# A recurrence's output gate in a PSUM bank and an activation of its own, with the 1 + o operation waiting for that activation, on one core

## What is computed

```python
x = x + L0_conv(ln_c(x))     # 7x7 involution: per-position kernels from two 1x1 convolutions
t = to_tokens(x);  t = t + L0_ffn(ln_t(t))   # 16 experts (64 -> 128 -> 64), the top 2 weighted
x = from_tokens(t);  x = x + L1_conv(ln_c(x))  # 3x3 convolution composed from low-rank terms
t = to_tokens(x);  t = t + L1_ffn(ln_t(t))   # a recurrence over the 3136 tokens:

def step(carry, xs):
    h, c = carry                      # each (4, 64)
    xi_t, xf_t, xg_t, xo_t = xs       # x_t @ U + b for every gate
    i_t = sigmoid(xi_t + h @ V_i)
    g_t = tanh(xg_t + h @ V_c)
    o_t = sigmoid(xo_t + h @ V_o)
    c_new = h * c + i_t * g_t         # gate f is not used
    h_new = o_t * tanh(c_new)
    return (h_new, c_new), h_new
```

## Time and profile before

| | |
|---|---|
| time, median of three | 3995.21 us |
| the profiled execution, its time | 3996.03 us |
| its span, first to last instruction | 3994.3 us |
| PE busy | 3584.6 us (90%) |
| DVE (VectorE) busy | 3374.4 us (84%) |
| ACT (ScalarE) busy | 2527.2 us (63%) |
| POOL (GpSimd) busy | 2156.5 us (54%) |
| recurrence steps | 3136 |

### The profile page before, as it was taken

The page is one execution under the profiler, slowest core; times in us unless marked ns, Lnnn a source line. Parts: engine busy times, 40 slices in busy tenths (PEclk is TensorE's granted clock), DMA queues, the critical chain, the costliest instruction groups (busy, mean ns, idle before and its releaser), DMA issues.

```text
span 3994.3 us, 130407 instructions
## 1 busy us (share of the span) xinstructions
PE 3584.6 (90%) x35548; PEld 2659.6 (67%) x35548; DVE 3374.4 (84%) x21816; ACT 2527.2 (63%) x11668; POOL 2156.5 (54%) x3179
## 2 busy tenths in 40 slices
PE   6899999989899999999999999999989899988888
PEld 5666666666666666666666666666666666666665
DVE  6688888888888888888888888888888888888887
ACT  4366666666666666666666666666666666666565
POOL 6655565656565656555555555565655565652222
PEclk7955555555555555555555555555555555555555
DMA  5000000000000000000000000000000000000000
GB/s 74 2 1 1 1 1 1 1 1 1 1 1 1 1 1 1 1 1 1 1 1 1 1 1 1 1 1 1 1 1 1 1 1 1 1 2 1 1 1 1
DMA packets 44538, 11.06 MB, mean 3 GB/s; under 512 B 39914, under 2 KB 44011, under 8 KB 44491
## 3 DMA queue, kind: packets, MB, share of 16 engines
q1 hardware_dynamic: 42378, 10.05, 1.6%
q10 hardware_dynamic: 2112, 0.46, 0.1%
HBM read 7.29 MB, written 3.21 MB: 3 GB/s over the span
## 4 chain that ended last, share of the span: by engine, by line
PE 66%; DVE 14%; ACT 13%; issue 5%; POOL 1%; DMA 0%; DVEq 0%; ACTq 0%; POOLq 0%
PE GATES L1343 14%; PE YB L1163 10%; PE GATES L1413 9%; ACT O L747 7%; PE H1B L1157 7%; ACT G L743 6%; DVE O L998 6%; PE YB L1314 6%; PE TAPB L1150 6%; PE DB L1282 5%; DVE HR L1002 5%; PE DB L1144 3%; PE H2B L1190 1%; PE H1B L1190 1%; PE H2B L1138 1%
## 5 line engine op out<-in xcount | busy, mean ns | idle before, releaser
L743 ACT ACTIVATE G<-GATES 128x12 f32<-128x12 f32 x3136 | 571.1, 182 | 1206.8 <-PE GATES L1413 1195.2
L1413 PEld LDWEIGHTS GATES<-HR,VW 128*128 128x128 f16 x6272 | 421.4, 107 | 601.5 <-issue 556.7
L1343 PE MATMUL GATES<-HR,VW 128*128 128x4 f16 x3136 | 531.8, 170 | 306.9 <-DVE HR L1002 214.0
L989 DVE TENSOR_TENSOR_SCAN CT<-G,CT 128x12 f32<-128x12 f32 x3136 | 586.5, 187 | 247.8 <-ACT G L743 218.7
L747 ACT ACTIVATE O<-G 128x8 f32<-128x8 f32 x3136 | 663.2, 211 | 98.7 <-ACT G L743 0.2
L998 DVE RECIPROCAL O<-O 128x4 f32<-128x4 f32 x3136 | 568.3, 181 | 175.1 <-ACT O L747 0.3
L1409 PEld LDWEIGHTS <-VW 128*128 128x128 f16 x3136 | 457.3, 146 | 354.3 <-issue 317.7
L976 DVE SCALAR_TENSOR_TENSOR CT<-HIST,CT 128x4 f32<-128x4 f32 x3136 | 522.0, 166 | 126.9 <-DVE HIST L1008 13.1
L1413 PE MATMUL GATES<-H,VB 128*128 128x4 f16 x6272 | 619.3, 169 | 0.0
L1413 PE MATMUL GATES<-HR,VW 128*128 128x4 f16 x6272 | 614.5, 168 | 0.0
L1163 PE MATMUL YB<-HD,W 128*64 128x112 f32 x3840 | 596.0, 412 | 1.7 <-DVE HD L869 1.7
(11 more groups left out here) (245 smaller groups left out, 6993.2 us busy)
## 6 DMA issues: line engine op xcount, KB each, us to landing
out_dram<-OUT SPq DMA_DIRECT2D x112, 28.0 KB, 1.9
X<-in_x_dram SPq DMA_DIRECT2D x4, 672.0 KB, 10.9
STG<-in_L_ffn_w_dram SPq DMA_DIRECT2D x4, 512.0 KB, 12.7
U<-in_L_conv_U2s_dram SPq DMA_DIRECT2D x1, 972.0 KB
W<-in_L_ffn_w_dram SPq DMA_DIRECT2D x1, 512.0 KB, 12.0
X<-in_x_dram ACTq DMA_DIRECT2D x4, 112.0 KB, 3.2
S<-in_L_conv_S1s_dram SPq DMA_DIRECT2D x1, 108.0 KB
S<-in_L_conv_S2s_dram SPq DMA_DIRECT2D x1, 108.0 KB
```

The costliest lines, as they stand in the source:

```text
L743: act.activation(G6[:, :, 2:5], gates[c][:, w, :, :], ACT.Tanh, scale=1 / GSCALE).then_inc(step_in, 1)
L989: dve.tensor_tensor_scan(CELL.rearrange("z b k -> z (b k)"), G6[:, :, :].rearrange("z b k -> z (b k)")[:, 0::2], ADD3.rearrange("z b k -> ...
L1343: return pe.add_instruction(mybir.InstMatmult(name=nc.get_next_instruction_name(), engine=mybir.EngineType.PE, start_tensor_calc=False, st ...
L1413: last = pe.matmul(gates[c][:, w, :, SLOT[g]], wt[:, g].rearrange("z m c -> z (m c)"), digit, start=False, stop=True, skip_group_check=True)
```

## The change

Gate o leaves the shared bank. Its inputs and its recurrent matmuls go into GATE_O, two slices of 112 columns of bank DB, in place of the third slice of GATES[0] and [1]; the order of the matmuls for each part of h becomes g, i, o (SLOT = (1, 0)). gates_done now counts after i, gate_o_done after o. ScalarE's L743 takes g and i alone (8 elements). A new activation takes tanh(o), 4 elements, from GATE_O to OT, four columns of the same bank, after the count step_in that stood ahead of L747 and after gate_o_done; 1 + o reads OT and waits for ot_done. Gate o's inputs are filled in by three prefills at place 5 for the second half of the row and at place 54 for the next row's first half, after 1 + o of that place (o1_done); the other six stand at place 3 and at places 51 to 53. As the prefill into DB no longer clears the bank in these rows, ScalarE zeroes a slice at places 1 and 49, and the first o matmul of the next place waits for it. The experts' weights move from DB into H1B, where expert H1 then waits for their copy (dbs_done) instead of for SI, and the spread norm factors move into H2B.

```diff
--- before.py
+++ after.py
...
         GAT=0, IXF=3, DM=((4, 5), (6, 8)), DT=(8, 9), DP=10, DPLO=11, DUPX=44, X4=47, DUP=54, XS=55, OUT3=54, OUT2=53,
-        PRE0={51: (0, 1, 2), 52: (3, 4), 53: (5, 6), 54: (7, 8)}, COPY=None, RSE=None)
+        PRE0={51: (0, 1), 52: (2, 3), 53: (4, 5)}, PRE0_O={54: (6, 7, 8)}, COPY=None, RSE=None)
 def head_places():
...
         GAT=0, IXF=0, DM=((0, 0), (0, 0)), DT=(1, 1), DP=2, DPLO=3, DUPX=50, X4=51, DUP=53, XS=54, OUT3=54, OUT2=54,
-        PRE0={55: tuple(range(9))}, COPY=5, RSE=23)
+        PRE0={55: tuple(range(9))}, PRE0_O={}, COPY=5, RSE=23)
 OUT_FREE_AT = (13, 48)
-PRODUCTS = 3 + 2 * 3
-PRE1_AT = {3: (0, 1, 2, 3, 4), 6: (5, 6, 7, 8)}
-SLOT = (2, 0, 1)
+INPUTS = (("b", 0), ("b", 1), (0, 0), (0, 1), (1, 0), (1, 1), ("b", 2), (0, 2), (1, 2))
+PRODUCTS = len(INPUTS)
+FIRST_O = INPUTS.index(("b", 2))
+PRE1_AT = {3: (0, 1, 2, 3, 4, 5), 5: (6, 7, 8)}
+ZERO_AT = (1, 49)
+SLOT = (1, 0)
 MAIN, HEAD = main_places(), head_places()
...
         TC5 = CT[:, 32:52].rearrange("z (b k) -> z b k", k=5)
-        gates = [g[:, 0:HALF * B * 3].rearrange("z (k b t) -> z t b k", b=B, k=3) for g in GATES]
+        gates = [g[:, 0:HALF * B * 2].rearrange("z (k b t) -> z t b k", b=B, k=2) for g in GATES]
+        GATE_O = [DB[:, c * TOK:(c + 1) * TOK] for c in range(2)]
+        gate_o = [g.rearrange("z (b t) -> z t b", b=B) for g in GATE_O]
+        OT = DB[:, 448:448 + B]
         REDF = TAPB[64:96, TOK:2 * TOK]
...
         def spread(lstm):
-            return DB if lstm else GATES[1]
+            return H2B if lstm else GATES[1]
+        def weights_bank(lstm):
+            return H1B if lstm else DB
         def logits(lstm):
...
                 act.wait_ge(hd_done, 1 + NG * j + k)
-                act.activation(DBS[:, :], DB[:, 0:EG * 2 * TOK], ACT.Copy).then_inc(dbs_done, 1)
+                act.activation(DBS[:, :], weights_bank(lstm)[:, 0:EG * 2 * TOK], ACT.Copy).then_inc(dbs_done, 1)
         def act_registers(act, j, t, involution):
...
             n = (j - LAG) * W + t
-            act.to_reg(1 + n + 1)
             if t < W - 1:
                 act.to_reg(1 + n + 2)
+                act.to_reg(1 + 2 * n + 4)
             if t == P.SQ:
...
                     act.wait_ge(gates_done, 1 + n + 1)
-                    act.activation(G6[:, :, 2:5], gates[c][:, w, :, :], ACT.Tanh, scale=1 / GSCALE).then_inc(step_in, 1)
+                    act.activation(G6[:, :, 2:5:2], gates[c][:, w, :, :], ACT.Tanh, scale=1 / GSCALE).then_inc(step_in, 1)
+                    act.wait_ge(step_in, 1 + 2 * n + 2)
+                    act.wait_ge(gate_o_done, 1 + n + 1)
+                    act.activation(OT[:, :], gate_o[c][:, w, :], ACT.Tanh, scale=1 / GSCALE).then_inc(ot_done, 1)
                     act_registers(act, j, t, involution)
-                    act.wait_ge(step_in, 1 + 2 * n + 2)
-                    act.activation(O5[:, :, 1:5:3], G6[:, :, 3:4].broadcast_to([128, B, 2]), ACT.Copy, scale=O_MAX, bias=1.0)\
-                        .then_inc(o1_done, 1)
+                    act.wait_ge(ot_done, 1 + n + 1)
+                    act.activation(O5[:, :, 1:5:3], OT[:, :].unsqueeze(2).broadcast_to([128, B, 2]), ACT.Copy, scale=O_MAX,
+                                   bias=1.0).then_inc(o1_done, 1)
                     act.wait_ge(cell_done, 1 + n + 1)
...
                         .then_inc(t_done, 1)
+                    for k in range(2):
+                        if t == ZERO_AT[k]:
+                            act.wait_ge(o1_done, 1 + n + 1)
+                            act.activation(GATE_O[1 - k], CST[:, CZERO:CZERO + 1].broadcast_to([128, TOK]), ACT.Copy).then_inc(oz_done, 1)
                 act_fill(act, j, t, involution, lstm, experts, pre)
...
-        def prefill(pe, c, k):
-            if k < 3:
-                return pe.matmul(GATES[c][:, SLOT[k] * TOK:(SLOT[k] + 1) * TOK], BX[:, k].rearrange("z m c -> z (m c)"),
-                                 ONEH[:, :], start=(k == 0), stop=False, skip_group_check=True)
-            d, g = divmod(k - 3, 3)
+        def prefill(pe, c, k, lstm):
+            d, g = INPUTS[k]
+            bank = GATE_O[c] if g == 2 else GATES[c][:, SLOT[g] * TOK:(SLOT[g] + 1) * TOK]
+            if d == "b":
+                return pe.matmul(bank, BX[:, g].rearrange("z m c -> z (m c)"), ONEH[:, :],
+                                 start=(k == 0 or (k == FIRST_O and not lstm)), stop=False, skip_group_check=True)
             xs = X4S[:, :].rearrange("z (p q w) -> z p q w", p=2, q=Q)[:, :, :, c * HALF:(c + 1) * HALF]
-            return pe.matmul(GATES[c][:, SLOT[g] * TOK:(SLOT[g] + 1) * TOK].rearrange("z (q p t) -> z p q t", q=Q, p=2),
+            return pe.matmul(bank.rearrange("z (q p t) -> z p q t", q=Q, p=2),
                              UX[:, d, g].rearrange("z m c -> z (m c)"), xs, start=False, stop=False, skip_group_check=True)
...
                         if lstm:
-                            pe.wait_ge(dbs_done, 1 + NG * j)
+                            pe.wait_ge(ve_done, 1 + 2 * j + 2)
                     last = spread_rs(pe, spread(lstm), 2 * k, 2 * k + 2)
...
                         pe.wait_ge(step_in, 1 + 2 * (j - LAG) * W)
-                    last = prefill(pe, 1, k)
+                    if k == FIRST_O:
+                        pe.wait_ge(o1_done, 1 + (j - LAG) * W + t + 1)
+                    last = prefill(pe, 1, k, lstm)
                     if k == PRODUCTS - 1:
...
                 k = P.H1.index(t)
-                pe.wait_ge(si_done, 1 + NG * j + k)
+                if lstm:
+                    pe.wait_ge(dbs_done, 1 + NG * j + k)
+                else:
+                    pe.wait_ge(si_done, 1 + NG * j + k)
                 if k == 0 and lstm:
...
                 if k == 0 and lstm:
-                    pe.wait_ge(ve_done, 1 + 2 * j + 2)
+                    pe.wait_ge(rsc_done, 1 + j + 1)
                 pe.wait_ge(v_done, 1 + 2 * NG * j + 2 * k)
...
                 if k == 0:
-                    if lstm:
-                        pe.wait_ge(rsc_done, 1 + j + 1)
                     pe.wait_ge(dp_step, 1 + 3 * j + 3)
...
                     for p in range(2):
-                        last = pe.matmul(DB[:, (2 * m + p) * TOK:(2 * m + p + 1) * TOK], SEL[:, p, EG * k + m, :], DP[:, :],
+                        last = pe.matmul(weights_bank(lstm)[:, (2 * m + p) * TOK:(2 * m + p + 1) * TOK], SEL[:, p, EG * k + m, :], DP[:, :],
                                          start=(m == 0 and p == 0), stop=True, skip_group_check=True)
...
                         pe.wait_ge(x4_done, 1 + j + 1)
-                    last = prefill(pe, 0, k)
+                    last = prefill(pe, 0, k, lstm)
                     if k == PRODUCTS - 1:
...
             if t == P.DUP:
-                if experts:
+                if experts and lstm:
+                    pe.wait_ge(dbs_done, 1 + NG * (j + 1))
+                elif experts:
                     pe.wait_ge(si_done, 1 + NG * (j + 1))
...
                     duplicate(pe, GATES[0], XD4).then_inc(dupx_done, 1)
+                for k in P.PRE0_O.get(t, ()):
+                    if k == FIRST_O:
+                        pe.wait_ge(o1_done, 1 + (j - LAG) * W + t + 1)
+                    last = prefill(pe, 0, k, lstm)
+                    if k == PRODUCTS - 1:
+                        last.then_inc(pre0_done, 1)
         def multiply_loaded(pe, out, weights, moving):
...
                         multiply_loaded(pe, gates[c][:, w, :, SLOT[0]], first, digit)
-                        for g in range(1, 3):
-                            last = pe.matmul(gates[c][:, w, :, SLOT[g]], wt[:, g].rearrange("z m c -> z (m c)"), digit,
-                                             start=False, stop=True, skip_group_check=True)
-                    last.then_inc(gates_done, 1)
+                        last = pe.matmul(gates[c][:, w, :, SLOT[1]], wt[:, 1].rearrange("z m c -> z (m c)"), digit,
+                                         start=False, stop=True, skip_group_check=True)
+                        if wt is VB:
+                            last.then_inc(gates_done, 1)
+                        if wt is VW and t - 1 in ZERO_AT:
+                            pe.wait_ge(oz_done, 1 + 2 * (j - LAG) + ZERO_AT.index(t - 1) + 1)
+                        last = pe.matmul(gate_o[c][:, w, :], wt[:, 2].rearrange("z m c -> z (m c)"), digit,
+                                         start=False, stop=True, skip_group_check=True)
+                    last.then_inc(gate_o_done, 1)
                 pe_fill(pe, j, t, involution, lstm, experts, pre)
...
```

More of the change, by code:

```diff
@@ L50 @@
 Places = namedtuple("Places", """MEAN MEAN_ORDER XC SQ VAR VE RSB RSC CONV1 RELU RED H1 SI H2 DB VV DBS HD W3 TAPA PA TAPD PROD CONV
-LOGIT LG MAX IDX NM TANH PW GAT IXF DM DT DP DPLO DUPX X4 DUP XS OUT3 OUT2 PRE0 COPY RSE""")
+LOGIT LG MAX IDX NM TANH PW GAT IXF DM DT DP DPLO DUPX X4 DUP XS OUT3 OUT2 PRE0 PRE0_O COPY RSE""")
 def main_places():
@@ L278, in build_program @@
```

(12 more changed lines are left out.)

## The result

The changed kernel takes 4318.89 us, the median of four runs (4316.59 to 4321.93), against 3995.23 (3995.12 to 3996.76). The ratio is 1.0811, 95% interval 1.0797 to 1.0824: 324 us slower. The forecast was 4282.

A forecast was written before the change was run, and what follows sets the result against it. The bound was 3136 turns of one serial loop, gates, cell, h, gates. Later L1005 0.117 less one matmul 0.026 gave 0.091 a turn, +285 us; with + 3, + 3 and - 4, 4282 us, range 4238 to 4385.

The forecast's parts named there:

- reserve on the o path: VectorE, before the change: the reciprocal's result is in at 0.675, L1005 starts at 0.71 behind HR; 0.035 us spare.
- The new last wait: VectorE: the reciprocal instead of HR releases L1005, which moves from 0.706 to 0.823, 0.117 us later a turn.
- the 0.82 ns an element: ScalarE: slope taken from L703 and L743, shortening L743 from 182 to 178.5 ns with 8 elements instead of 12.
- the bound of 1 + o: ScalarE: 1 + o taken as 178 ns, bounds 167 and 211; at 211 it adds 33 ns a turn, 4385 us.
- Tanh(o)'s own bound of 182 ns: ScalarE: tanh(o) from PSUM to PSUM taken as 158.5 ns, bounds 155 and 182.
- the second count's 0.03: ScalarE: tanh(o)'s second wait, gate_o_done, was put at nothing, with a bound of 0.03 us.
- Banks, prefills, H1's wait: PE and the bank work: bank moves and H1's wait cost nothing, prefills at places 5 and 54 3 us.
- VectorE's RED: VectorE's filler makes the next scan 0.09 late, 0.03 more x 50 rows; with DPLO + 3 us.
- A: ScalarE: tanh(o) starts 0.07 behind L743 without waiting for its end; -0.03 a turn, 3901 us; chance 0.04.
- B: ScalarE: L750 starts only when 1 + o has ended; 0.057 more than forecast, 4461 us; chance 0.04.
- C: ScalarE: the split gives no earlier start, L743 still follows the third matmul; +0.026, 4364 us; chance 0.05.
- D: ScalarE: a short activation has one fixed cost wherever its operands lie; + 137, 4419 us; chance 0.06.

The follow-up runs named there:

- e9: The kernel before the change, with tanh(c) taking its zero bias from a column in SBUF instead of as an immediate: 4238.63 us.
- e8: The changed kernel, with tanh(c) taking its zero bias from a column in SBUF instead of as an immediate: 4328.14 us.
- e3: The changed kernel with OT, the result of tanh(o), in SBUF instead of PSUM: 4466.12 us.
- e5: The changed kernel with only its bank and place moves: three gates share one bank and one tanh, nothing zeroed: 3994.17 us.
- e6: Against e1: 1 + o waits for ot_done, then h_done of the step before instead of step_in, with one register instruction less: 3948.17 us.
- e1: The changed kernel with the wait for step_in moved from ahead of tanh(o) to ahead of 1 + o, before ot_done: 4123.29 us.
- e2: The changed kernel with L755 (tanh of g and i) waiting for gate_o_done instead of gates_done: 4425.9 us.
- e7: Against e6: the register work moved behind the activation of 1 + o: 3947.94 us.

## Why the prediction was right

**The bound.** The loop of 3136 turns, and 0.035 us of reserve on the o path, were read rightly. e9 shows that before the change tanh(c) carries its whole lengthening into the time. The reserve is what the reciprocal lost (0.457 to 0.615) less what H5 lost (0.705 to 0.831): 0.158 - 0.126 = 0.032.

**The new last wait.** The step on which the forecast rests, L1005 going over from HR to the reciprocal, is what the profile after shows, and e8 beside e9 proves it. The start of 1 + o was put at 0.40 and is at 0.40; its length at 178 ns and is 179; tanh(o)'s at 158.5 and is 158. One fixed cost for a short activation does not fit: the same tanh(o) takes 158 ns into PSUM and 174 into SBUF (e3).

**What was too small.** The measured time is 37 us above the forecast. The median turn grew by 0.104 and not by 0.091, and 0.013 x 3136 is 41 us. Two terms make it up. H5 starts 0.126 later and not 0.117: L755 takes 181 ns, not 178.5, and the hand-overs are 0.032 to 0.033, not 0.03, so the reciprocal stands at 0.615 instead of 0.607. Behind H5 the turn got 0.022 shorter (0.502 to 0.480) and not 0.026: H5 takes 196 ns instead of the 188 before the change (0.19 in the earlier trace rows), and its first matmul comes 0.248 behind its start instead of 0.240. Four fewer elements saved 1 ns in L755 (182 to 181) and not 3.5: the 0.82 ns an element, worked out from L703's 539 ns for 448 elements, doesn't hold between 12 and 8.

**The range and the signs.** The top of the range, 4385, has the bound of 1 + o alone in it. Tanh(o)'s own bound of 182 ns would have added 74 us and the second count's 0.03 another 94, so the range was narrower than the bounds that the prediction names. One of its signs did not come: PE busy was to fall to some 0.85 and is 0.89. The same number of matmuls adds up to 3855.9 us of busy time instead of 3584.6; why was not followed. H5 stands 0.12 behind HR and not 0.14, because HR queues behind the reciprocal.

**What was set aside.** Banks, prefills, H1's wait: put at 0 to 3 us, and e5 finds nothing in the kernel with three gates in one bank; in the changed kernel places 0 and 15 of the row are late by 1 and 2 us in all. VectorE's RED was put at 3 us with DPLO, and that was wrong in kind. The timeline of VectorE at that place in the changed kernel, as the earlier trace rows:

```profile
2042.28 0.27 DVE L847 SCALAR_TENSOR_TENSOR RED<-TAPB,RED 32x112 f16<-32x112 f32 x1
2042.58 0.19 DVE L1010 TENSOR_TENSOR_SCAN CT<-G,CT 128x12 f32<-128x12 f32 x1
2042.90 0.18 DVE L1019 RECIPROCAL O<-O 128x4 f32<-128x4 f32 x1
2043.00 0.16 DVE L1023 SCALAR_TENSOR_TENSOR HR<-O,CT 128x4 f16<-128x4 f32 x1
2043.11 0.20 DVE L1026 TENSOR_TENSOR_SCAN H<-O,CT 128x20 f16<-128x20 f32 x1
```

L755 of that step starts at 2042.28, so the scan is at 0.30 instead of 0.22, and H5 still at 0.83: a late scan falls into the reserve that the cell path has got. The turns bear it out: at place 8, whose scan stands behind RED, the filler of place 7, the turn is 1.260 before against 1.207 elsewhere, 1.311 as everywhere in the changed kernel, and 1.262 against 1.187 in e6, where the reserve is gone again.

**The rivals.** A (faster, if tanh(o) isn't held) was not what this change does, but it was the right condition. The forecast had its saving as 0.03 a turn and 3901 us; with the hold taken away and ot_done carried by 1 + o itself it is 0.02 in a plain turn, and 3948. What neither it nor the expectation of e1 had is the 0.06 us a turn between e1, where ot_done comes last and is waited for by an instruction of its own (1 + o at 0.338), and e6, where 1 + o carries it (0.278). B (ScalarE closed by 1 + o) is out: L766 starts 0.08 behind L763's start, 0.10 before its end. C is out by e2, D by e3.

## What to carry to other kernels

The split started a chain one matmul earlier, and that was worth 0.034 us a turn here (e2). What decided was how much reserve the other chain had into which the new instruction went, here 0.035 for a cost of 0.16. Look at what a new instruction waits for. Tanh(o) waited for a count that its data doesn't need and that L755, just ahead of it on its own engine, raises: it started at 0.213 with that wait (the changed kernel) and at 0.074 without (e1), and with the wait moved from tanh(o) to 1 + o 196 of the 324 us were gone. In e6, where step_in is not waited for at all and 1 + o carries the late ot_done itself, the same split took 3948.17 us, 1.2% less than before the change. See in the trace, too, which wait an instruction with two of them carries itself. In e1 the late one was the separate instruction: 4123.29 us, 3.2% more than before the change and 175 more than e6. The two differ in one register instruction as well, whose removal from ahead of 1 + o gained nothing in e7 against e6 (3947.94).

## What the runs showed of the hardware

- Tanh(o) started 0.074 us behind the start of the activation ahead of it (L755, 181 ns long) in e1 and e6, where no count held it, but for place 6 with 0.205. In the changed kernel, where it carried step_in, which that activation raises, it started at 0.213, 0.032 behind its end.
- Of the two waits ahead of tanh(o) (the changed kernel) or 1 + o (e1) the second in the source was an instruction of its own in 3136 of 3136 turns, and of those ahead of 1 + o in e6 and e7 in 3080; in the other 56, at place 0, a register instruction carried the first and 1 + o the second. 1 + o started 0.03 us behind tanh(o)'s end where it carried the wait for it (0.278, e6 and e7), 0.09 behind where the separate instruction had it (0.338, e1), and 0.11 behind where the register instruction had it (0.356, place 0 of e6 and e7).
- Register instructions that carried no wait (35 to 80 ns each in e1) did not move 1 + o: it started at 0.403 with one or two of them behind tanh(o)'s start and at 0.402 with none (the changed kernel), and at 0.278 with one ahead of tanh(o)'s start (0.040, e6) or with none (e7).
- The place of a short activation's operands: 158 ns PSUM to PSUM (the changed kernel), 174 PSUM to SBUF (e3) for four elements; with eight written, 179 from PSUM to SBUF (the changed kernel) and 211 from SBUF to SBUF (e3 and before).
- Tanh(c) took 242 ns with its bias from a column in SBUF (e9) against 162 without (the kernel before), and 239 (e8) against 173 (the changed kernel).
- The scan H5 is recorded with 188 ns in the kernel before, and with 196 in the changed kernel and in e1, e2, e3, e6, e7 and e8, in which gate o has its own activation, also where it starts 0.08 behind HR as before (e6, e8). Why was not found out.
